# Language-model tower on one core: factor rows and batch 0's factor kept on chip, expert weight splitting inside the first turns, every third comparison on ScalarE, third expert layer moved

## The reference

```python
# 1 token features: a running count of each skill, and of its correct answers, up to t
tup  = [skill * skill_w + skill_b, attempts * att_w + att_b, correct / max(attempts, 1) * mast_w + mast_b]
h    = where(valid, tup @ proj_w.T + proj_b, 0)                     # 64 wide
# 2 attention with a decaying state, d = 64, n = 256
x_update = relu(v_prev @ Dx.T)
x_t   = 0.97 * x_state + x_update;  x_t /= max(sum(abs(x_t)), 1e-12)
a_star = rho @ x_t;  y_t = relu(ln(a_star) @ Dy.T) * relu(x_t)
v_star = ln(y_t @ E.T);  rho = 0.97 * rho + ln(v_prev) x_t^T
h = h + v_star
# 3 mixture of 8 experts, top 2, evaluated densely: hidden 128, gelu
logits = xn @ Wr + br;  w = softmax(top 2)
h = h + sum_e w_e * (gelu(xn @ W1[e] + b1[e]) @ W2[e] + b2[e])
```

## Time and profile before

| | us |
|---|---|
| median of 3 runs | 782.51 (782.14 to 783.56) |
| profiled execution, its own time | 784.06 |
| span of its trace | 782.2 |
| TensorE busy | 665.1 (85%) |
| VectorE busy | 610.7 (78%) |
| ScalarE busy | 358.8 (46%) |
| GpSimd busy | 283.4 (36%) |
| mean granted clock of TensorE | 0.954 |

### The profile page before, as it was taken

One profiled execution on the slowest core, in us unless ns is written; L12 is line 12 of the kernel. 1 busy time (PEld: TensorE's weight loads), 2 busy tenths in 40 slices (PEclk: granted clock), 3 DMA queues, 4 the chain that ended last, 5 costly groups with the idle time before them and its releaser, 6 DMA issues.

```text
span 782.2 us, 16874 instructions
## 1 busy us (share of the span) xinstructions
PE 665.1 (85%) x4030; PEld 375.4 (48%) x4062; DVE 610.7 (78%) x2531; ACT 358.8 (46%) x819; POOL 283.4 (36%) x333
## 2 busy tenths in 40 slices
PE   2663993257799999999999999999999999999876
PEld 0552662134455555555555555555555555555432
DVE  5998887766778888888888888888888888887752
ACT  4000994002255555555554455555545554555543
POOL 1000000012234445555444444445555544444443
PEclk9999997568899999999999999999999999999988
DMA  7000000010333333333444433333333444432223
GB/s 243 31 0 0 1 0 11 4 60 28 87 104 90 89 88 88 88 89 89 106 104 101 111 104 88 88 88 88 88 89 88 103 103 105 107 108 62 62 62 75
DMA packets 45186, 61.06 MB, mean 78 GB/s; under 512 B 21560, under 2 KB 24108, under 8 KB 44652
## 3 DMA queue, kind: packets, MB, share of 16 engines
q1 hardware_dynamic: 43028, 60.13, 29.8%
q10 hardware_dynamic: 1944, 0.66, 0.4%
q0 software_dynamic: 192, 0.01, 0.0%
HBM read 55.77 MB, written 5.02 MB: 78 GB/s over the span
## 4 chain that ended last, share of the span: by engine, by line
PE 72%; DVE 12%; issue 6%; ACT 4%; POOL 2%; DMA 1%; DVEq 1%; SPq 0%; ACTq 0%; POOLq 0%
PE bank L1170 18%; PE bank L1268 13%; PE bank L1261 7%; PE bank L1262 6%; PE bank L1182 5%; PE bank L1209 5%; PE bank L1226 4%; PE bank L1286 3%; ACT skill_rows L511 3%; DVE same L667 3%; PE bank L1103 2%; PE bank L1114 1%; PE bank L1159 1%; PE bank L1218 1%; PE bank L1235 1%
## 5 line engine op out<-in xcount | busy, mean ns | idle before, releaser
L511 ACT ACTIVATE skill_rows<-bank,b1T,w_scale 128x512 f32<-128x512 f32 x256 | 194.6, 775 | 84.0 <-PE bank L1262 83.0
L1170 PE MATMUL bank<-feat_parts 128*128 128x256 f32 (+3 forms) x512 | 160.8, 449 | 4.7 <-DVE feat_parts L837 4.6
L1268 PE MATMUL bank<-skill_rows,w_sb 128*64 128x512 f32 x256 | 121.2, 594 | 0.2
L1269 PE MATMUL bank<-skill_rows,w_sb 128*64 128x512 f32 x256 | 121.2, 594 | 0.0
L1170 PEld LDWEIGHTS bank<-feat_parts 128*128 128x128 f32 x512 | 91.0, 194 | 47.1 <-issue 21.2
L387 POOL TENSOR_TENSOR t_z<-t_z,power 128x4 f32<-128x4 f32 x32 | 32.5, 1017 | 188.4 <-DVE t_z L884 188.4
L484 ACT ACTIVATE feat_parts<-bank 128x384 f32<-128x384 f32 (+2 forms) x96 | 36.8, 384 | 134.2 <-DVE feat_parts L843 134.2
L408 POOL TENSOR_TENSOR feat_parts<-skill_rows 128x512 f32<-128x512 f32 x64 | 81.3, 1270 | 17.9 <-DVE skill_rows L970 17.9
L375 POOL TENSOR_TENSOR same<-h_all,mean_h 128x256 f32 (+1 forms) x32 | 19.6, 612 | 164.5 <-DVEq L1034 164.4
L837 DVE TENSOR_TENSOR_SCAN feat_parts<-same,feat_parts 128x512 f32<-128x512 f32 x64 | 74.6, 1207 | 0.0
L393 POOL TENSOR_TENSOR h_scale<-t_h,power 128x4 f32<-128x4 f32 x32 | 32.6, 1018 | 109.7 <-DVE t_h L915 109.7
(11 more groups left out here) (252 smaller groups left out, 1286.8 us busy)
## 6 DMA issues: line engine op xcount, KB each, us to landing
same<-factor_d SPq DMA_DIRECT2D x32, 512.0 KB, 3.8
skill_rows<-w_d SPq DMA_DIRECT2D x32, 512.0 KB, 6.1
feat_parts<-w_d SPq DMA_DIRECT2D x32, 512.0 KB, 6.1
skill_rows<-skill_row_d SPq DMA_DIRECT2D x4, 1024.0 KB, 7.7
out<-o_sb SPq DMA_DIRECT2D x32, 128.0 KB, 6.3
w_sb<-in_L_ffn_W ACTq DMA_DIRECT2D x2, 256.0 KB
w_d<-wT SPq DMA_DIRECT2D x32, 16.0 KB, 1.4
table_k<-table_d SPq DMA_DIRECT2D x9, 2.5 KB
```

What stands on the lines that cost most here:

```text
L511: act.activation(hid[:, e, :], h_bank[e % 2][:, :], ACT.Gelu, bias=b1T[:, e:e + 1], scale=w1_scale[:, e:e + 1]).then_inc(ac_gelu, 1)
L1170: last = pe.matmul(n_bank[sc % 2][:, 0:WIDE[sc]], xs[:, k, sc * P:(sc + 1) * P], xs[:, k, sc * P:S], start=(k == 0), stop=(k == NK - 1))
L1268: pe.matmul(z_bank[q % 2][0:D, :], w2_sb[:, 2 * q, :], hid[:, 2 * q, :], start=True, stop=True)
L1269: pe.matmul(z_bank[q % 2][D:P, :], w2_sb[:, 2 * q + 1, :], hid[:, 2 * q + 1, :], start=True, stop=True)\
```

## The change

- Compare stage: batches are taken in ten triples and two single ones. VectorE compares batches 3j and 3j+1 as before; ScalarE compares batch 3j+2 as relu(1 - (row - skill)^2) with four Square instructions and one Relu, into `same_a` (which lies over `h_all`), and VectorE multiplies only its diagonal blocks (`own_only`). VectorE first clears `same_a` and writes the negated ids.
- Glue: TensorE transposes the row sums straight into the [32, 512] layout in PSUM, and `upd_d`, its store and its two loads are gone. The row operations come before the weights' preparation and read `row_u`, `row_rstd` from PSUM. Batch 0's factors are spread to 128 partitions by two matmuls with `first` (a row of ones in a zero matrix), and `first_scan` reads them from PSUM; `load_factor` starts with batch 1.
- `u_scale` is computed on GpSimd with `pow`. ScalarE copies `eT` and `dyT` out of PSUM and makes batch 0's relu. GpSimd sets the constants.
- Expert weights: `expert_scale` after `first_scan`, `router_weights` in turn 0, `expert_parts` in turn 1, the transposes (`expert_parts_T`) and `expert_weights` in turn 2.
- In every turn with expert work `hidden(k, 2)` stands between `scores(i, 2)` and `scores(i, 3)`.

```diff
@@ SyncE
-            sp.wait_ge(updT_in, 1)
-            sp.dma_start(upd_d, upd_T[:]).then_inc(st_upd, 16)
-            sp.wait_ge(st_upd, 16)
-            for n, row in enumerate((row_u, row_rstd)):
-                sp.dma_start(row.rearrange("b (c p) -> b c p", p=P), ...).then_inc(ld_row_u, 16)
-            sp.wait_ge(factors_in, 1)
+            sp.wait_ge(factors_in, 2)
...
-            load_factor(0)
@@ GpSimd
+                pool.wait_ge(var_in, 1)
+                pool.tensor_scalar(u_scale[:], var_h0[:], 1.0 + EPS, EPS * EPS, ALU.mult, ALU.add)
+                pool.tensor_tensor(u_scale[:], u_scale[:], power_j[:], ALU.pow)
+                pool.tensor_tensor(scales, scales, dec..., ALU.mult).then_inc(scales_in, 1)
@@ ScalarE
+            def equal(j, side):
+                wait(act, pe_counts, 3 * (j - 1))
+                for sc in range(C):
+                    act.activation(same_a[side][:, 0:C - sc, sc, :],
+                                   skill_rows[:, bass.ds((3 * j + 2) * S + sc * P, WIDE[sc])]...,
+                                   ACT.Square, bias=neg_T[:, ...]).then_inc(gap_sq, 1)
+                act.wait_ge(gap_sq, C * (j + 1))
+                used = same_a[side].rearrange("p j c n -> p (j c n)")[:, 0:3 * S + P]
+                act.activation(used, used, ACT.Relu, bias=1.0, scale=-1.0).then_inc(gap_is, 1)
...
+            act.activation(eT[:]..., bank[5][:, P:2 * P], ACT.Copy).then_inc(ac_ed, 1)
+            act.activation(dyT[:], bank[4][:, 0:NS], ACT.Copy).then_inc(ac_ed, 1)
+            for k in range(NK):
+                act.wait_ge(pe_pre, k + 1)
+                act.activation(relu_b[:, k, :], n_bank[k][:, :], ACT.Relu).then_inc(ac_row, 1)
@@ VectorE
+            dve.memset(h_all[:].bitcast(BF16)[:, 0:2 * C * S], 0.0).then_inc(neg_in, 1)
+            dve.tensor_scalar(neg_T[:], skill_T[:], -1.0, None, ALU.mult).then_inc(neg_in, 1)
...
-            def equal(b, side):
-                wait(dve, pe_counts, b - 1)
+            def equal(b, side, n):
+                wait(dve, pe_counts, b - 2)
...
+            def own_only(n, side):
+                dve.wait_ge(gap_is, n + 1)
+                own = same_a[side][:, 0]
+                dve.tensor_tensor(own, own, upto_b..., ALU.mult).then_inc(same_in, 1)
+            def three(j, side):
+                equal(3 * j, 0, 2 * j)
+                equal(3 * j + 1, 1, 2 * j + 1)
+                own_only(j, side)
...
-            dve.wait_ge(pe_updT, 1)
-            dve.tensor_copy(upd_T[:]..., bank[1][:, 0:2 * P]).then_inc(updT_in, 1)
+            dve.wait_ge(rows_set, 3)
+            dve.wait_ge(pe_updT, 1)
+            op(dve.tensor_scalar(row_nz, row_u, 0.0, None, ALU.is_gt))
+            op(dve.tensor_tensor_scan(row_any, row_nz, row_zero, 0.0, ALU.max, ALU.add))
+            op(dve.tensor_scalar(row_w, row_u, grow, DECAY, ALU.mult, ALU.min))
+            op(dve.scalar_tensor_tensor(row_w[:, 3:S], row_any[:, 0:S - 3], DECAY, row_w[:, 3:S], ALU.mult, ALU.max))
+            op(dve.tensor_scalar(row_one[:, 3:S], row_any[:, 0:S - 3], -grow, grow, ALU.mult, ALU.add))
+            op(dve.tensor_tensor_scan(row_past[:, 1:S + 1], row_one, row_w, 0.0, ALU.mult, ALU.add))
+            op(dve.scalar_tensor_tensor(row_d, row_past[:, 0:S], DECAY, row_u, ALU.min, ALU.add))
+            op(dve.tensor_scalar(row_d, row_d, L1_EPS, None, ALU.max))
+            op(dve.reciprocal(row_w, row_d))
+            dve.wait_ge(pe_updT, 2)
+            dve.tensor_tensor(row_any, row_w, row_rstd, ALU.mult).then_inc(factors_in, 1)
+            dve.tensor_scalar(row_nz, row_w, DECAY, None, ALU.mult).then_inc(factors_in, 1)
+            dve.tensor_scalar(w1g[:], w1_sb[:], gam2[0:D, 0:1], None, ALU.mult).then_inc(gammas_in, 1)
...
+            def first_scan():
+                dve.wait_ge(pe_row, 1)
+                dve.wait_ge(ac_row, NK)
+                for k in range(NK):
+                    dve.tensor_tensor(relu_b[:, k, :], relu_b[:, k, :], bank[7][:, :], ALU.mult)
+                dve.wait_ge(pe_row, 2)
+                for k in range(NK):
+                    dve.tensor_tensor_scan(xs[:, k, :], bank[3][:, :], relu_b[:, k, :], 0.0, ALU.mult, ALU.add)
...
+                if isinstance(i, int) and i == 1:
+                    expert_parts()              # before diagonal(i, 0)
+                if isinstance(i, int) and i == 0:
+                    router_weights()            # after diagonal(i, 3)
+                if isinstance(i, int) and i == 2:
+                    expert_weights()            # after scan(i + 1)
...
-            scan(0)
-            (u_scale by rsqrt, wait pe_parts, two copies of w1k)
+            first_scan()
+            expert_scale()
@@ TensorE
+            pe.wait_ge(upd_in, 1)
+            for values_t, rows in ((upd_sum, row_u), (rstd, row_rstd)):
+                for c in range(C):
+                    last = pe.transpose(rows[:, c * P:(c + 1) * P], values_t[:]...[:, c], ident_f[:])
+                last.then_inc(pe_updT, 1)
...
+                pe.matmul(bank[7][:, :], first[:], row_any, start=True, stop=True).then_inc(pe_row, 1)
+                pe.matmul(bank[3][:, :], first[:], row_nz, start=True, stop=True).then_inc(pe_row, 1)
...
+                if mlp:
+                    hidden(k, 2, 1 - side)
+                if att:
                     scores(i, 3)
-                if mlp:
-                    hidden(k, 2, 1 - side)
...
+                if isinstance(i, int) and i == 2:
+                    expert_parts_T()            # before update(i + 1)
...
             update(0)
+            biases()
+            first_factor()
+            expert_T()
```

More of the change, by code:

```diff
@@ L52 @@
 N_RES = 23
+TRIPLES = B // 3
 N_MLP = 14
@@ L145, in program @@
         stat_g = sb("stat_g", [P, 2, GROUP, 6])
-        upd_sum, upd_T = sb("upd_sum", [P, J]), sb("upd_T", [J, 2, P])
+        upd_sum = sb("upd_sum", [P, J])
+        first, power_j = sb("first", [B, P]), sb("power_j", [P, J])
         h_all = sb("h_all", [P, J * D])
+        same_a = [h_all[:].bitcast(BF16)[:, n * C * S:(n + 1) * C * S].rearrange("p (j c n) -> p j c n", j=C, c=C)
+                  for n in range(2)]
+        neg_T = newton
         skill_rows = sb("skill_rows", [P, J * P], BF16)
@@ L1083, in count, with of_dve, of_act, three @@
                 last.then_inc(pe_counts, 1)
-            pe.wait_ge(tok_in, 1)
-            with pe.Fori(0, B // 2) as pair:
-                count(2 * pair, 0)
-                count(2 * pair + 1, 1)
+            def of_dve(side):
+                return lambda sc, tc: same[:, side, sc * S + P * tc:sc * S + P * tc + P]
+            def of_act(side):
+                return lambda sc, tc: same_a[side][:, tc - sc, sc, :]
+            def three(j, side):
+                count(3 * j, of_dve(0))
+                count(3 * j + 1, of_dve(1))
+                count(3 * j + 2, of_act(side))
+            pe.wait_ge(tok_in, 1)
+            three(0, 0)
+            three(1, 1)
+            with pe.Fori(1, TRIPLES // 2) as two:
+                three(2 * two, 0)
+                three(2 * two + 1, 1)
+            for n in range(B - 3 * TRIPLES):
+                count(3 * TRIPLES + n, of_dve(n))
             def features(g, side):
@@ new lines, in biases @@
+            def biases():
+                pe.wait_ge(ld_w3, 16 * 6)
+                pe.wait_ge(ac_ed, 2)
+                for e in range(E):
+                    pe.matmul(bank[5][:, e:e + 1], w1_sb[:, e, :], bet[:], start=True, stop=True)
+                pe.wait_ge(wide_beta, 1)
+                pe.matmul(bank[5][:, E:2 * E], bet_wide[:], wr_sb[0:D, :], start=True, stop=True)
+                pe.transpose(bank[5][:, 16:24], b1_sb[:], ident_f[0:E, 0:E])
+                pe.transpose(bank[5][:, 24:24 + NP], b2_sb[:], ident_f[0:NP, 0:NP]).then_inc(pe_bias, 1)
```

248 lines of the change are left out of this document (138 added, 110 removed).

## The result

Over four runs each, the changed kernel took 766.12 us (760.67 to 766.44), the kernel before 782.79 us (782.14 to 783.56): a ratio of 0.9764 (95% interval 0.9743 to 0.9784). The forecast was 763.5 us in a range of 751 to 771. The profiled execution of the changed kernel took 766.28 us with a span of 764.4; the sum of the prediction, made against a profiled execution, said 765.0. Against the medians the forecast is 2.6 us off, against the profiled execution 1.3.

The account below looks back on a forecast made before the run. VectorE was taken to bound compare stage and glue, TensorE with one hole the steady turns. -6.5 - 16.0 + 2.9 + 0.5 = -19.1 from 784.06 gave 765.0, less 1.55 to the median, 763.5 us; 80% range 751 to 771.

Parts of the forecast that it names:

- Compare stage: Comparisons before the glue: ScalarE takes one batch in three and paces triples at 3.6 us; -6.5 us.
- Glue: From row sums to first scores: no round trips through device memory, weights' work moved; scores at 149.5, not 165.46; -16.0 us.
- `pow`: `u_scale` on GpSimd ahead of the first `values`: takes 29 us against 28 of cover; +1.0 us, bounds 0 and 5.
- The other moved work: Expert-weight preparation moved into the first turns, partly hidden there; +1.9 us.
- the w1k copies: Turn 0: copies that pushed the first diagonal block late go away; -0.5 us.
- Case E: Clock near the first scores: glue's new matmuls raise it earlier or let it fall; 2 us either way, no chance given.
- Moved layer: Steady turns, `hidden(k, 2)` earlier: TensorE's gain is waited away at `fold`; -0.07 to +0.12 us per turn, +0.5 us taken.
- the hole's 13.5 us: TensorE's waits ahead of `hidden(k, 4)` for the third gelu, 0.52 us a turn, 26 times between 240 and 720 us.
- rival D: Steady turns at `fold`: later `diagonal(i, 3)` delays it, slower than before; decides from 0.66 us per turn; chance 0.04.
- A: Steady turns: TensorE's hole is gained in full, about 12.5 us less, 751 us, period near 17.6; chance 0.12.
- B: Compare stage: ScalarE's comparisons don't pay, 4.3 us a triple or more, or counts don't fit; 770 us; chance 0.10.
- C: Moved work not hidden: `pow` at its upper end, 4 more, and fill turns, 2 more; 769.5 us; chance 0.12.

Follow-up runs that it names:

- experiment 9: Changed kernel with a second, unused `pow` over 128 columns ahead of the first on GpSimd: 782.02 us, ratio 0.9979 to the kernel before.
- kernel 1: Changed kernel with the third expert layer put back, `hidden(k, 2)` behind `scores(i, 3)` again: 757.68 us, ratio 0.9681 to the kernel before.
- kernel 2: Kernel before with only the third expert layer moved, `hidden(k, 2)` ahead of `scores(i, 3)`: 785.57 us, ratio 1.0026 to the kernel before.
- kernel 4: Changed kernel with GpSimd's two adds for `fold` placed ahead of the centring: 783.42 us, ratio 1.0001 to the kernel before.
- kernel 3: Kernel before with GpSimd's two adds for `fold` placed ahead of the centring: 805.83 us, ratio 1.0289 to the kernel before.
- kernels 5, 6 and 7: Changed kernel with `fold` behind `attn_var`; behind `attn_var` and `hidden(k, 6)`; the latter with the third layer put back: 752.58, 747.73 and 761.62 us.

## Why the prediction was right, and where it was off

- **Compare stage, -6.5 booked, -8.3 measured.** The mechanism was right, the triple was sized too long: 3.43 us where I took 3.6. The third triple started at 22.70 where I had 23.3, and the last eight took 28.3 us, one wait included, where I had 28.8. And 0.5 of the difference is a slip of the booking: my own working ends at 56.4 against 63.4, which is -7.0, and I booked -6.5 without a reason. The four Squares take 1.90 us (my 1.76 and 0.14 of the 0.52 that I allowed for the bias), the Relu 1.59 (1.56 forecast), and they overlap a little, 3.43 for 3.49, where I had added handoffs. The clearing took 1.76 us (1.75), and VectorE's first comparison came at 18.93 (18.9). It was ScalarE that paced the triples: from 30.33 on its instructions follow each other without a gap, and ahead of that it waited once, 0.66 us, for TensorE's counts; VectorE waited for TensorE's counts in three of them (0.31, 0.48 and 0.36 us). The stage ended at 55.19 where I had 56.4.
- **Glue, -16.0 booked, -15.9 measured.** From the start of `upd_sum` at 124.05 to the scores at 142.15 it is 18.1 us, where the prediction has 149.5 - 131.5 = 18.0, with the same start at 131.50 in the kernel before. In the seven other kernels that keep this glue it takes 18.10 to 18.12 us. The row operations ran from 125.54 to 135.84, 10.3 us against 10.2; the first row stood in PSUM 2.2 us later (2.0), the scores 4.1 after that (4.1). The first source in PSUM costs as a two-source operation does (0.68), as taken.
- **`pow`, +1.0 booked, 0 measured.** It took 20.82 us, inside my bounds of 1.3 and 33 but not the 29 that I took. Four columns cost 1.02, 128 cost 20.82: 19.8 us for 124 columns more, 160 ns per column, and some 0.4 us fixed if the cost is linear in between. I had put nearly all of the 1.02 on the columns. Its cover was 27 us by experiment 9 (20.8 + 6.5), where I worked out 28.
- **The other moved work, +1.9 booked, +0.95 in turns 0 to 3.** It depends on the clock. Turn 0, booked at -0.5 for the w1k copies, is 0.6 shorter at a clock of 0.89 (15.54 us in kernel 1, 16.16 in kernel 2, which has none of the moved work), but not at 0.71 (16.62 in the changed kernel, 16.41 before). In turn 1 at full clock it is +0.8 (14.54 us in kernel 4, 13.77 in kernel 3, which differ by the whole change), beside the 0.7 that I booked for `expert_parts`. In turn 2 it is nothing at full clock (15.20 us in kernel 1, 15.21 in kernel 2) and +1.4 where the clock fell within the turn: 17.73 at 0.81 in the changed kernel, 16.31 at 0.79 in the kernel before; kernels 5, 6 and 7 repeat the first with 17.7, kernel 3 the second with 16.31. The rows show the mechanism. The sixteen transposes of turn 2 at half clock, the product of the next batch that had to wait behind them, and that product in the kernel before:

```profile
185.54 1.87 PE L1282 MATMUL bank<-ident_h,w_p 128*128 128x128 f16 x16
187.97 1.29 DVE L921 SCALAR_TENSOR_TENSOR feat_parts<-bank,same 128x512 f32<-128x512 f32 x2 [1.78 <-remote]
209.95 1.29 DVE L833 SCALAR_TENSOR_TENSOR feat_parts<-bank,same 128x512 f32<-128x512 f32 x2 [0.20 <-remote]
```

  VectorE stands idle for 1.78 us instead of 0.20. At full clock, in kernel 1, the transposes take 1.05 us and the product waits 0.35: there they are hidden. I had the 0.9 to 1.9 us of the transposes right and put +0.7 between the two cases. `expert_weights`, booked at +1.0, costs nothing: turn 3 takes 17.29 us in kernels 1 and 7, which have it, and in the kernel before. The -0.38 of turn 3 in the table is the moved layer's. Case E had the clock vary in turn 0 by the glue's new matmuls; in the profiled execution turn 0 ran at 0.71 as before.
- **Moved layer, +0.5 booked, +3.6 in the turns measured.** The prediction was right that the hole's 13.5 us would not be had, and why: TensorE waits at `fold` for what it gained (0.26 became 0.86). It was the size within -0.07 to +0.12 per turn that was off. The scores that start a turn of the kernel before, `h_var` and the weights of `fold` in it, and then the start of a turn of 18.12 us of the changed kernel and its `fold`:

```profile
411.81 1.96 PE L1170 MATMUL bank<-feat_parts 128*128 128x512 f32 x4
418.46 0.16 DVE L915 SCALAR_TENSOR_TENSOR t_h<-t_h 128x4 f32<-128x4 f32 x1
423.79 0.97 PEld L1286 LDWEIGHTS bank<-fold_f,feat_parts 128*128 128x128 f32 x8 [0.26 <-POOL feat_parts L413]
409.07 1.96 PE L1301 MATMUL bank<-feat_parts 128*128 128x512 f32 x4
421.12 1.10 PE L1421 MATMUL bank<-fold_f,feat_parts 128*128 128x64 f32 x8 [0.27 <-POOL feat_parts L444]
```

  From the start of a turn `diagonal(i, 3)` comes at 5.90 us instead of 5.78 (417.59 in the earlier trace rows) in both kinds of turn: that is the 0.1 that I had worked out. In the turns of 18.12 us the delay stays small, and `fold` comes at 12.05 instead of 11.98; these turns are 0.05 longer than before, inside my range. In those of 18.29 us `h_var` comes at 6.89 instead of 6.65 and `fold` at 12.21, and they are 0.22 longer. The record doesn't show why the delay grows in every second turn only. In the mean a turn lengthens by 0.13, just past my upper bound. This is the way of rival D, at a fifth of the 0.66 that it needed. Kernels 1 and 2 put the move at 4.3 and 2.2 us over these turns, so that the 3.6 is its price to within about 1 us.
- **Rivals.** A is excluded as the profile stands: a period of 18.21 us and not 17.6. Its gain was real, though, and lay one edit away (17.69 us, 0.38 below the kernel before and most of the 0.43 of A). B is excluded by the period of 3.43, C by the 20.82 us of `pow` and by turns 0 to 3, which are 0.95 us longer in all and not at the upper end of 5.

So the bounds, the waits and the places were as predicted, but that the total came out only 1.3 us beside the profiled forecast is luck: -1.8 (compare) and -1.0 (`pow`) stood against +3.1 (moved layer), and the +0.85 between the stages and +1.0 after the last turn's start, neither of which I had booked, against turns 0 to 3 that were 0.95 cheaper. These two I did not follow to an instruction. Between the same two markers kernels 2 and 3, which have the code of the kernel before there, take 68.6 and 68.5 us against its 68.0 and the changed kernel's 68.9, so that most of the +0.85 need not be the change's; and kernel 1 takes 0.5 us less than the changed kernel after the start of its last turn. Open, too, is what sets the clock in turns 0 to 2: kernels with the same code there differ by 4 us, and the executions of one kernel differ among themselves (760.67 to 766.44 us for the changed one, at mean clocks of 0.969 and 0.963), but only one of each was profiled.

## What to carry to other kernels

An engine's hole is worth its time only if no closed loop through other engines is as long as the turn: follow the next wait behind the hole back until it comes to the same engine again, and move what lies on that stretch and needn't (here 0.42 us of `attn_var`, which gave 0.42 us per turn) together with the edit that fills the hole. A turn that lacks one link of the loop, as turn 3 lacks `fold`, shows what the edit gives without it. Before moving work on GpSimd, look at what VectorE does at the new place. Price work that is moved into a stretch of varying clock at both levels, with the slack at either. And read an early stage's saving at its own marker, since a total of a kernel whose first turns run at one clock or the other can hide 3 us.

## What the runs showed of the hardware

- Two 128x512 f32 additions on GpSimd beside four 128x64 `scalar_tensor_tensor` with two SBUF sources on VectorE: these took 2.15 us instead of 0.86. The two that met an addition ended 0.08 us after it (560 and 1283 ns instead of 268 and 280), the two between took 272 ns each; of GpSimd's additions the first kept its 1.27 us, the second took 1.33 instead of 1.27. MAX8 with one source (155 ns) and a `tensor_tensor` with one of its sources in PSUM (0.29 us) were not held up.
- `pow` on GpSimd: 1.02 us for 4 columns, 20.8 for 128, three times alike (20.82, 20.81, 20.77), each time on the same data.
- The granted clock of the first turns differs between profiled executions of kernels whose instructions there are the same: 0.81 and 1.00 in turn 2, 17.72 and 15.20 us. TensorE was granted 2.4 GHz throughout in the one and 1.2 GHz for part of the turn in the other. In turns 0 and 1 it was 0.71 and 0.91 in the changed kernel, 0.89 and 1.00 in kernel 1.
- A memset of 4096 bf16 issued as 2048 uint32 took 1.76 us, the 0.82 ns per element of the small ones in the earlier trace rows and no more.
